# Router weights carried beside the rows, one-hots on VectorE, and three changes of order in a two-layer attention, expert and RWKV kernel

## The reference

```python
# x: 1 x 2048 x 512
x = x + attn(layernorm(x))     # causal, 16 heads of 32: softmax(q k.T / sqrt(32)) v, then w_out
x = x + ffn(layernorm(x))
x = x + rwkv(layernorm(x))
x = x + ffn(layernorm(x))      # the same weights again

def ffn(x):
    s = sigmoid(x @ gate_w)                  # 32 experts, 4 groups
    # experts of 2 groups are left (by the groups' maxima), of them the 6 best are chosen
    w = s[chosen] / sum(s[chosen])
    return sum_k w_k * expert_k(x) + shared(x)   # silu(x g) * (x u) @ d, widths 352 and 704

def rwkv(x):                                 # xk, xv, xr: mixes of a row and the row before
    k, v, r = xk @ key_w.T, xv @ value_w.T, xr @ receptance_w.T
    # over the 2048 rows, for each of 512 channels
    p = max(pp, u + k); y = (exp(pp-p)*aa + exp(u+k-p)*v) / (exp(pp-p)*bb + exp(u+k-p))
    p2 = max(pp + w, k); aa, bb = (exp(pp+w-p2)*t + exp(k-p2)*g for t, g in ((aa, v), (bb, 1)))
    return (sigmoid(r) * y) @ output_w.T
```

## Time and profile before

| | |
|---|---|
| three runs | 3811.81, 3827.97, 3828.18 us; median 3827.97 |
| the profiled execution | 3811.86 us, span 3809.6 us |
| granted TensorE clock, mean | 0.929 |
| busy: PE, DVE, ACT, POOL | 88%, 55%, 42%, 29% of the span |
| DMA moved | 379 MB |

### The profile page before, as it was taken

How to read it: one execution, slowest core, us unless ns; L and a number is a source line. 1 busy time by engine, 2 the same in 40 slices (tenths; PEclk the granted TensorE clock), 3 DMA queues, 4 the chain that set the end, 5 groups by cost and what they waited for, 6 DMA issues and landing times. The chain is left out here.

```text
span 3809.6 us, 61820 instructions
## 1 busy us (share of the span) xinstructions
PE 3370.4 (88%) x16308; PEld 2533.8 (67%) x16309; DVE 2097.7 (55%) x3549; ACT 1584.8 (42%) x2090; POOL 1089.8 (29%) x841
## 2 busy tenths in 40 slices
PE   7899999999788879999999958858887999998996
PEld 6644444444565668888888823327655888888886
DVE  4265555551465455555555558766553555555554
ACT  2134444443210145555555555522011555555553
POOL 0100000000223234444444423312232444444443
PEclk9889999999698989999999978977888999999998
DMA  4501111201300056666665520032002566665554
GB/s 166 146 10 35 35 36 43 51 9 56 107 23 12 17 176 165 162 150 166 167 168 147 101 102 22 23 120 78 19 12 98 158 165 166 169 157 148 145 145 104
DMA packets 108270, 379.03 MB, mean 99 GB/s; under 512 B 14000, under 2 KB 14768, under 8 KB 96176
## 3 DMA queue, kind: packets, MB, share of 16 engines
q1 hardware_dynamic: 55536, 253.66, 19.9%
q0 software_dynamic: 52608, 123.76, 16.9%
HBM read 277.49 MB, written 104.07 MB: 100 GB/s over the span
## 5 line engine op out<-in xcount | busy, mean ns | idle before, releaser
L1522 DVE TENSOR_TENSOR g_lo<-g_raw,g_hi x232 | 562.8, 2426 | 431.3 <-ACT g_hi L1469 393.4
L1424 POOL DMA_INDIRECT acc_rows<-g_y,g_ids x232 | 411.8, 1775 | 876.6 <-DVE g_ids L1532 367.1
L1469 ACT ACTIVATE g_hi<-g_raw x232 | 469.7, 2025 | 431.5 <-issue 325.8
L540 DVE TENSOR_REDUCE b_part_max<-b_p_rows 128x1 f32<-128x512 f32 (+3 forms) x640 | 375.0, 609 | 307.2 <-PE b_p_rows L601 154.4
L514 ACT ACTIVATE b_probs<-b_p_cols 128x1024 f32<-128x1024 f32 (+1 forms) x320 | 282.4, 898 | 385.5 <-PE b_p_cols L621 199.4
L1415 POOL DMA_INDIRECT g_rows_in<-xn_rows,g_ids x240 | 337.2, 1405 | 88.6 <-issue 88.0
L1574 PE MATMUL g_p_gate<-g_hi,g_rows_hi 128*128 x928 | 324.3, 349 | 37.6 <-issue 27.5
L1574 PE MATMUL g_p_gate<-g_hi,g_rows_lo 128*128 x928 | 303.6, 327 | 0.0
L1574 PE MATMUL g_p_gate<-g_lo,g_rows_hi 128*128 x928 | 303.5, 327 | 0.0
L598 PE MATMUL b_p_rows<-b_k_stack,b_q_stack 96*128 96x512 f32 (+3 forms) x640 | 275.7, 458 | 30.0 <-DMA b_k_stack<-qk_hi 18.5
L1574 PE MATMUL g_p_up<-g_hi,g_rows_hi 128*128 x928 | 299.0, 322 | 0.0
(11 more groups left out here) (315 smaller groups left out, 6743.8 us busy)
## 6 DMA issues: line engine op xcount, KB each, us to landing
g_raw<-in_expert_weights_dram SPq DMA_DIRECT2D x64, 2176.0 KB, 8.9
acc_rows<-f_acc SPq DMA_DIRECT2D x34, 256.0 KB, 2.0
qk_hi<-a_hi SPq DMA_DIRECT2D x32, 256.0 KB, 2.6
qk_lo<-a_lo SPq DMA_DIRECT2D x32, 256.0 KB, 2.9
b_q_stack<-qk_hi SPq DMA_DIRECT2D x32, 256.0 KB
b_k_stack<-qk_hi SPq DMA_DIRECT2D x32, 256.0 KB
xn_rows<-f_xn SPq DMA_DIRECT2D x8, 1024.0 KB, 5.5
a_x<-in_x_dram SPq DMA_DIRECT2D x4, 1024.0 KB
```

The source lines that it names most:

```text
L540: v.tensor_reduce(part_max[:, h, t % BT, c:c + 1], p_rows[:, u % NROWB, 0:w], AX.X, ALU.max).then_inc(rows_free, 1)
L1424: pool.indirect_dma_start(out=acc_rows, out_offset=bass.IndirectOffsetOnAxis(ap=ids[:, i:i + 1].bitcast(U32), axis=0), in_=y[:, n, :], in_ ...
L1469: act.activation(hi[:, bass.ds(place, PIECE)], raw[:, bass.ds(source, PIECE)], ACT.Copy).then_inc(split_hi_ready, 1)
L1522: v.tensor_tensor(lo[:, bass.ds(place, PIECE)], raw[:, bass.ds(source, PIECE)], hi[:, bass.ds(place, PIECE)].bitcast(F32), ALU.subtract).t ...
```

## The change

1. **Attention.** `mask_t` and its products (L624) go. Instead GpSimd writes zeros over the masked half of `probs` after ACT's exp, on each of the 16 diagonal steps of a pair, one instruction for both heads; `products` of such a step waits for it. The copy of the next pair's values stands behind the fourth of them.
2. **Router, early part.** Block 0 gets its statistics alone, blocks 1 to 3 together. A block is turned into four PSUM banks instead of two. Gate logits have the gate weights as stationary operand (4 products of 512 columns a block), are copied by ACT and turned back. The low part of `wdown` is computed by VectorE. In the second layer the rows are loaded in four pieces inside the router; the load stage goes.
3. **Router weights.** sigmoid and normalisation are computed on all 32 logits of a row, masked by `taken`, and SyncE stores them beside the row: `xn_rows` has 544 columns, and a gather brings 2176 B a row instead of 2048 B. `scale_y` reads its factor from the gathered row, at the tile's expert, which costs ACT a value load more.
4. **One-hots.** Both by VectorE; `tile_hot` holds one table of 160 columns instead of three, the ring has 8 places, and the one-hots of a group are made a group ahead of `multiply`.
5. **RWKV.** `output(n - 3)` stands behind `project(n, R_)`, and `add_out(b - 1)` moves from behind unit 2's fraction in block b to before unit 3's.

```diff
@@ attention, GpSimd @@
+                    for m in DIAGONAL:
+                        pool.wait_ge(probs_ready, n * NSTEP + m + 1)
+                        pool.sem_inc(mask_order, 1)
+                        pool.affine_select(out=probs[:, m % NPROB, :, 0:P], in_=probs[:, m % NPROB, :, 0:P], compare_op=ALU.is_ge, fill=0.0,
+                                           base=0, pattern=[[0, HPAIR], [1, P]], channel_multiplier=-1).then_inc(masked, 1)
+                        if m == last_step[0] and not is_last(n):
+                            if not is_first(n):
+                                pool.wait_ge(probs_free, n * NSTEP + NPROB)
+                            take_values(n + 1, 1 - i)
@@ attention, TensorE @@
                         mm = pe.matmul(p_cols[:, m % NCOL, h, 0:BW - d], k_stack[i][h][0:NROW, kt * P:(kt + 1) * P],
-                                       q_stack[i][h][0:NROW, j * BW + d:(j + 1) * BW], start=True, stop=kt < j * BT)
-                        if kt >= j * BT:
-                            mm = pe.matmul(p_cols[:, m % NCOL, h, 0:P], ident_b[:], mask_t[:], start=False, stop=True)
+                                       q_stack[i][h][0:NROW, j * BW + d:(j + 1) * BW], start=True, stop=True)
...
-                    pe.wait_ge(probs_ready, n * NSTEP + m + 1)
+                    if m in DIAGONAL:
+                        pe.wait_ge(masked, n * len(DIAGONAL) + DIAGONAL.index(m) + 1)
+                    else:
+                        pe.wait_ge(probs_ready, n * NSTEP + m + 1)
@@ router @@
-        NR = 4
+        NR = 8
-        tile_hot = sb("tile_hot", [P, NR, 3, TILES], F32R)
+        tile_hot = sb("tile_hot", [P, NR, TILES], F32R)
...
+                    for b in range(NB):
+                        sp.dma_start(resid[:, b * BT:(b + 1) * BT, :], resid_in[:, b * BT:(b + 1) * BT, :]).then_inc(resid_loaded[b], 16)
...
+                sp.wait_ge(weights_ready, 1)
+                sp.dma_start(rows(xn_rows[0:T, D:D + E]), weight[:]).then_inc(weights_stored, 16)
@@ router, VectorE @@
+                v.wait_ge(down_hi_ready, 2)
+                v.tensor_tensor(wdown_lo[:, 0:FULL, :], wdown[:, 0:FULL, :], wdown_hi[:, 0:FULL, :].bitcast(F32), ALU.subtract).then_inc(down_lo_ready, 1)
...
-                chain.link(v.reciprocal(score[:], score[:]))
+                chain.link(v.tensor_scalar(weight[:], weight[:], 1.0, None, ALU.add))
+                chain.link(v.reciprocal(weight[:], weight[:]))
+                chain.link(v.tensor_tensor(weight[:], weight[:], taken[:], ALU.mult))
+                chain.link(v.tensor_reduce(weight_sum[:], weight[:], AX.X, ALU.add))
@@ router, TensorE @@
-                            m = pe.matmul(p_logits[:, t, :], xT_f[:, b % 2, c, t % BT * P:(t % BT + 1) * P], wg[:, c, :], start=(c == 0), stop=(c == KD - 1))
+                        pe.wait_ge(xTf_ready, b * KD + c + 1)
+                        m = pe.matmul(p_mm[0:E, 2 + b % 2, :], wg[:, c, :], xT_f[:, b % 2, c, :], start=(c == 0), stop=(c == KD - 1))
@@ experts, ACT @@
-                    act.activation(y[:, n, :], p_y[:, i, :], ACT.Copy, scale=disp.row_weights[:, bass.ds(t, 1)]).then_inc(y_ready, 1)
+                    expert = at_tile(act, disp.tile_expert, t, E - 1)
+                    weight = rows_in[:, slot, D:D + E][:, bass.ds(expert, 1)]
+                    act.activation(y[:, n, :], p_y[:, i, :], ACT.Copy, scale=weight).then_inc(y_ready, 1)
@@ RWKV, VectorE @@
+                    if c == 3 and 1 <= b < NB:
+                        add_out(b - 1)
                     if n >= 2:
                         fraction(n - 2)
-                    if c == 2 and 1 <= b < NB:
-                        add_out(b - 1)
@@ RWKV, TensorE @@
-                    if n >= 3:
-                        output(n - 3)
                     project(n, K_)
...
                     project(n, R_)
+                    if n >= 3:
+                        output(n - 3)
```

More of the change, by code:

```diff
@@ L341, in stage_attention @@
     NSTEP = len(steps)
+    DIAGONAL = [m for m, (j, kt) in enumerate(steps) if kt >= j * BT]
     assert len(row_steps) == NSTEP
@@ L1037, in _ @@
                         if i == 0 and f == 2:
[L1038 to L1039 removed]
+                            act.wait_ge(logits_read, 1)
+                            act.activation(weight[:], logits[:], ACT.Exp, scale=-1.0).then_inc(exp_ready, 1)
                     high_hidden(i, FULL)
@@ L2066, in build @@
         k.end_stage()
-        resid_loaded = k.sem("resid_loaded")
-        def load(resid):
-            with nc.Block() as block:
-                @block.sync
-                def _(sp):
-                    sp.dma_start(resid[:], rows(time_mixed)).then_inc(resid_loaded, 16)
-                    sp.wait_ge(resid_loaded, 16)
-        second_rows = layer(2, load)
+        second_rows = layer(2, None, time_mixed)
         out_stored = k.sem("out_stored")
```

215 lines of the change are left out of this document (125 added, 90 removed).

## The result

The changed kernel takes 3592.95 us (median of four runs, 3588.78 to 3594.22), the kernel before 3822.11 (four runs, 3811.81 to 3828.18). The ratio is 0.9401, with a 95% interval of 0.9375 to 0.9427: 6% faster. The profiled execution took 3592.62 us, with a span of 3590.6, where the one before had 3811.86 and 3809.6. 3620 us had been forecast, in a range of 3575 to 3690.

What follows compares the result with a forecast made beforehand. Bounds were set by stage: TensorE in attention, TensorE and VectorE alternating in RWKV, stalls in the shared expert, TensorE near a tie with the adds among experts. -17 - 38 - 41 - 106 + 8 = -194 gave 3618, called 3620 us; range 3575 to 3690.

Steps and rivals of the forecast that it cites:

- Attention: Attention: 256 mask products leave TensorE and GpSimd's select hides behind matmuls; -17 us, bounds 0 and -30.
- RWKV: Recurrence: projections no longer wait behind y, so VectorE's idle time for K goes; -38 us, bounds -20 and -55.
- The quarter that I left in for `add_out`: Recurrence: a quarter of VectorE's idle time stays, since add_out waits for outputs issued a unit's projections later.
- Early parts: Router before the first up product: it starts sooner; -16 us in the first layer, -25 in the second.
- Shared experts: Router's shared expert: stalls for GpSimd's row one-hots go as VectorE makes them; -53 us a layer, -106 in all.
- Experts: Expert stages: wider gathers lengthen the chain of adds, ACT's value load hides; +8 us for both layers.
- (a): Shared expert: VectorE becomes the bound and 48 us of gain stay out; 3668 us, chance 0.2.
- (b): Recurrence: RWKV keeps its pace, TensorE and VectorE still alternating; -10 instead of -38, 3648 us, chance 0.12.
- (c): Attention: GpSimd's select takes over 1.5 us, so nothing is gained or 5 lost; 3640 us, chance 0.12.
- (d): Experts: wider gathers or ACT's value load come onto the path, slower than before; 3875 us, chance 0.03.
- (e): Shared expert: other stalls of the same size follow, little of the 106 comes; 3720 us, chance 0.04.
- The signs: Expected in the changed profile: table waits under 1 us, shared expert 245, up after 48, VectorE's K waits under 15.

Runs made afterwards that it cites:

- e13: The kernel before with the attention part of the change alone: 3809.20 us, ratio 0.9969 to the kernel before.
- e7: The changed kernel with GpSimd's select over the masked half made twice on each diagonal step: 3595.70 us.
- e9: The changed kernel with the whole RWKV part put back (output ahead of the projections, add_out behind the third unit's fraction): 3631.43 us.
- e2: The changed kernel with add_out alone put back behind the fraction of a block's third unit, output staying behind the projections: 3593.65 us.
- e8: The changed kernel with GpSimd starting the low part of the up weights only after all 16 row tiles are normalised: 3579.76 us.
- e3: The changed kernel with row one-hots made by GpSimd at their old place ahead of hidden_lo, ring of eight kept: 3745.66 us.
- e4: The changed kernel with a ring of four one-hots instead of eight: 3590.84 us.
- e10: The changed kernel with gathered rows of 2048 B again, no weights' store, router weights left out of the result: 3590.19 us.
- e6: The changed kernel with 576 columns a row instead of 544 (2304 B), so every row starts on a multiple of 256 B: 3597.67 us.
- e5: The changed kernel with ACT scaling every tile by column 512, without its value load of the tile's expert: 3592.51 us.
- e11: e8 with RWKV's last multiplication of the fraction moved from VectorE to GpSimd, with two buffers for the denominator: 3588.58 us.
- e12: e8 with RWKV's addition of the top term moved from GpSimd to VectorE: 3583.77 us.

## Why the prediction was right, point by point

The forecast was 3620 us, 27 above the median of 3592.95; the range held it, and "faster" at 0.95 came out. Against the profiled execution the sum was -194, and -219 came. Part of this closeness is luck: the shared experts gave 38 us more than their term, the early parts gave 3 us less and the experts took 11 us more, so the misses partly cancel. Attention and RWKV came within 3 us of their terms.

- **Attention**: -17 forecast, -16.2, and -15.2 in e13. The select is 0.41 us, inside my bounds of 0.28 and 1.0, and e7 shows that the cover holds.
- **RWKV**: -38, and -40.4. The circle was read right: e9 brings 35.8 us of it back with the same waits. The quarter that I left in for `add_out` had the wrong reason, since e2 shows that its place costs nothing; what is left in is VectorE's own work. Part of it has grown: its product `r_delta` takes 1.38 us on average in the changed kernel and 0.94 in e9.
- **Early parts**: -16 and -25, and -14.4 and -23.2. VectorE's being held by GpSimd, taken from L132 beside L963, was the right choice, and e8 shows it. The Trainium skill, SBUF — State Buffer, section "Who interferes with whom", has it that the two share a port pair under an exclusive lock. The traces agree: 17.23 us for twelve normalisations beside GpSimd and 5.66 without it (e8), and the difference is two of them that last as long as GpSimd's 6.87 and 5.61 us. I had blocks 2 and 3 held once, to 1004 us in the trace of before, which is 25.3 us after the stage's start; they were held twice, and block 2's turn began 31.4 after it. From there to the first `up` I had 22.5 us and 18.2 came. The term came out because these two misses, 6.1 and 4.3 us, nearly cancel.
- **Shared experts**: -106 forecast, -143.8 measured. This is the term that was mis-sized, by 38 us. The mechanism is as said: GpSimd's one-hots at their place (e3 brings all of it back), not the ring (e4). Two steps of the sum were too dear. "Three turns 11" was priced at the low clock: sixteen turning products take 1.9 us at full speed (48 in 5.9 us), so 6. "96 tables under 19": four tables of 160 columns take 0.40 us, so 10. My ideal was 229 and should have been 215. And "I leave 14 us in" was too much: the waits that came are 3.4 us for the tables, and some low clock stands behind them and at the start. 215 and 9 are the 224 measured.
- **Experts**: +8 forecast, +19.3 measured. Some 7 of these are the late gather that the first stage of the profile before was without; some 6 in the first stage have no known cause and may be chance. The mechanism of the term, a longer chain of adds behind wider gathers, has no support: narrow rows (e10) don't bring the first stage back, and some 2 us are left in the second. By the Trainium skill, DMA: Bandwidth & Descriptors, section "How a descriptor splits into AXI transactions", I had 9 or 10 transactions for a row and so +25. That was miscounted: by that section's rule a row of 2176 B is 9 transactions wherever it starts (8 of 256 B and one of 128, or 9 counted from the boundary below), where one of 2048 B is 8. The estimate would be gathers 12.5% longer and, by the same sum, +18. No trace here shows such a cost, with 4.4 us for the median gather and 4.3 in e10; and e6 can't test the odd starts by that rule, since a row of 2304 B is 9 transactions too.
- **The rivals**: (a) VectorE as the bound of the shared expert: no, 139 of 225 us busy in it, and after the first one-hots no product of TensorE waits over 0.2 us for it. (b) RWKV at its pace, no. (c) the slow select, no. (d) slower through the experts, no; the value load is free (e5). (e) other stalls in place of the old ones, no.
- **The signs**: `up` starts 49.7 us after the stage (48 said), the shared expert takes 224 (245 said), VectorE's wait for K is 0.4 (under 15 said). One product of the tables waits over 1 us, the first, with 2.93; the sum had it, the sign had none. The first layer's experts took 17.3 us more, close to the 20 at which I'd have called the forecast wrong.

## What to carry to other kernels

When one engine's queue mixes short work that others wait for with work that waits for others, moving the short work to another engine's queue can be worth far more than its duration: GpSimd's 0.64 us one-hots cost 72 us a layer at the place where they stood, a deeper ring changed nothing, and only half of it was waiting: the rest went with TensorE's lower clock behind the stalls. Put the product that waits for a late result behind the ones that feed the engine making it. And look for a short instruction of VectorE that lasts as long as the one of GpSimd beside it (here L132, and two of the normalisations L138): one wait that puts GpSimd's long work behind took another 17 us from the two early parts, 13 from the run.

## What the runs showed of the hardware

- VectorE's twelve normalisations of 128x512 took 17.23 us beside two GpSimd subtractions of 6.87 and 5.61 us, and 5.66 when these came after. Only two of the twelve were long, 6.94 and 5.79 us, the ones that came just behind the start of one of GpSimd's; one that was under way when GpSimd's began was not. GpSimd was hardly slowed: its two took 12.30 us in e8 and 12.48 beside VectorE.
- In RWKV, VectorE's reciprocal keeps its 3353 ns in all fourteen profiles, while of its products and scans some get longer with more work on GpSimd (the scan 1.52 to 1.89 us in e11) or shorter with less (`below` 1.37 to 0.68 in e12). GpSimd's product with v gets longer too, 1.96 to 2.48 in e11.
- After a stall of 3.22 us TensorE's `up` products started 0.43 us apart in e3, where they start 0.23 apart at full clock; after one of 5.05 us among the experts four turning products took 1.11 us instead of 0.60.
- The 77th gather of a stage lands late in 26 of 28 expert stages, and such a stage is some 7 us longer. Two profiles of stages whose code is the same can differ by this much. A comparison of two single profiles must allow for that before it blames the change.
